# Argmax cross-attention kernel: index of fifteen chunks taken ahead, gathers by row tile, ternary weights in two passes

## The reference, cut to what matters

```python
qp = jnp.einsum('bld,ed->ble', q, Wq)             # 512 rows
scores = jnp.einsum('bld,bmd->blm', qp, kv)       # 512 x 8192
idx = jnp.argmax(scores, axis=-1)
mem = jnp.take_along_axis(kv, idx[..., None], axis=1)
mkv = jnp.einsum('bld,ed->ble', mem, Wkv)
mk, mv = jnp.split(mkv, 2, axis=-1)
...
qh = qp.reshape(b, l, h, dh).transpose(0, 2, 1, 3)
logits = jnp.einsum('bhld,bmd->bhlm', qh, mk) * scale
attn = jax.nn.softmax(logits, axis=-1)
...
def weight_quant(w):
    scale = 1.0 / jnp.clip(jnp.mean(jnp.abs(w)), 1e-05)
    return jnp.clip(jnp.round(w * scale), -1, 1) / scale
```

## Time and profile before

| | before |
|---|---|
| median of 3 runs | 1133.74 us (1131.56 to 1134.1) |
| span of the profiled execution, first to last instruction | 1129.8 us |
| PE busy, share of the span | 1047.0 us, 93% |
| DVE busy | 819.6 us, 73% |
| POOL busy | 416.9 us, 37% |
| share of PE in the chain that ended last | 70% |
| mean granted TensorE clock | 0.980 |

### The profile page before, as it was taken

How to read it: one execution, slowest core, us unless ns; L and a number is a source line. 1 busy time by engine, 2 the same in 40 slices (tenths; PEclk the granted TensorE clock), 3 DMA queues, 4 the chain that set the end, 5 groups by cost and what they waited for, 6 DMA issues and landing times.

```text
span 1129.8 us, 14853 instructions
## 1 busy us (share of the span) xinstructions
PE 1047.0 (93%) x4981; PEld 495.9 (44%) x4981; DVE 819.6 (73%) x1178; ACT 489.2 (43%) x731; POOL 416.9 (37%) x229
## 2 busy tenths in 40 slices
PE   7999999999999989999479999999997799888997
PEld 3444444444444444544134444444642145466453
DVE  5476666799999376685973399999477557476896
ACT  2345554666666537146771110100034615255163
POOL 5177778200000644000020377767128920084003
PEclk9999999999999999999779999999999999999998
DMA  6145545533433345320010435546100010000001
GB/s 237 75 132 194 184 160 166 201 112 121 147 140 112 142 157 224 111 93 1 0 75 6 148 142 200 188 170 188 37 1 1 8 70 1 1 1 1 2 1 38
DMA packets 41830, 112.64 MB, mean 100 GB/s; under 512 B 4512, under 2 KB 15296, under 8 KB 35648
## 3 DMA queue, kind: packets, MB, share of 16 engines
q1 hardware_dynamic: 38592, 101.13, 25.5%
q10 hardware_dynamic: 2880, 9.96, 2.6%
q0 software_dynamic: 320, 1.05, 0.3%
HBM read 103.18 MB, written 7.34 MB: 98 GB/s over the span
## 4 chain that ended last, share of the span: by engine, by line
PE 70%; DVE 17%; ACT 5%; issue 3%; DMA 2%; POOL 2%; DVEq 0%; SPq 0%; ACTq 0%; POOLq 0%
PE PS L773 5%; PE PS L1647 5%; PE PS L1649 5%; PE PS L775 5%; PE PS L1648 5%; PE PS L774 5%; PE PS L804 5%; PE PS L805 5%; PE PS L806 5%; PE PS L255 3%; PE PS L256 3%; PE PS L257 3%; DVE arena L1998 2%; DMA arena<-in_w 2%; DVE arena L1574 2%
## 5 line engine op out<-in xcount | busy, mean ns | idle before, releaser
L773 PE MATMUL PS<-arena 128*128 128x512 f16 x256 | 97.0, 379 | 2.0 <-DVE arena L622 2.0
L1647 PE MATMUL PS<-arena 128*128 128x512 f16 x256 | 97.0, 379 | 1.8 <-DVE arena L1531 1.8
L804 PE MATMUL PS<-arena 128*128 128x512 f16 x256 | 97.0, 379 | 0.9 <-DVE arena L695 0.9
L774 PE MATMUL PS<-arena 128*128 128x512 f16 x256 | 97.0, 379 | 0.0
L775 PE MATMUL PS<-arena 128*128 128x512 f16 x256 | 97.0, 379 | 0.0
L1648 PE MATMUL PS<-arena 128*128 128x512 f16 x256 | 97.0, 379 | 0.0
L1649 PE MATMUL PS<-arena 128*128 128x512 f16 x256 | 97.0, 379 | 0.0
L806 PE MATMUL PS<-arena 128*128 128x512 f16 x256 | 97.0, 379 | 0.0
L805 PE MATMUL PS<-arena 128*128 128x512 f16 x256 | 97.0, 379 | 0.0
L629 DVE TENSOR_TENSOR arena<-PS,arena 128x512 f32<-128x512 f32 x64 | 43.6, 681 | 58.0 <-ACT arena L553 58.0
L249 PE MATMUL PS<-IDENTB 128*128 128x512 bf16 x225 | 60.5, 416 | 21.9 <-DVE SM L1259 21.9
(11 more groups left out here) (370 smaller groups left out, 2439.8 us busy)
## 6 DMA issues: line engine op xcount, KB each, us to landing
arena<-in_ctxT SPq DMA_DIRECT2D x32, 1024.0 KB, 6.3
arena<-in_ctx SPq DMA_DIRECT2D x16, 1024.0 KB, 5.4
arena<-in_w ACTq DMA_DIRECT2D x8, 1024.0 KB, 5.2
arena<-in_w SPq DMA_DIRECT2D x8, 1024.0 KB, 4.8
XN<-in_ffnGU SPq DMA_DIRECT2D x16, 384.0 KB, 3.4
XN<-in_WinT SPq DMA_DIRECT2D x16, 290.0 KB, 5.1
gu_hi<-arena SPq DMA_DIRECT2D x16, 192.0 KB, 3.4
gu_lo<-arena SPq DMA_DIRECT2D x16, 192.0 KB, 3.5
```

The costliest lines, as they stand in the source:

```text
L773: pe.matmul(bank, CHI[:, b, e, cols], QHI[:, e, :], start=(e == 0), stop=False)
L774: pe.matmul(bank, CHI[:, b, e, cols], QLO[:, e, :], start=False, stop=False)
L804: pe.matmul(PS[:, t, :], PHI[:, j, cols], CHI[:, b, j, :], start=False, stop=False)
L1647: pe.matmul(bank, QHI3[:, e, cols], CHI3[:, b, e, :], start=(e == 0), stop=False)
```

## The change

- The last pair of the DVE loop is written out behind it. The reduction over `TOPV` and `TOPI` now takes 15 chunks and stands ahead of the last chunk's maxima. In the last chunk each tile gets its maximum, its place and three operations of one column that merge it with the result of the 15 chunks; each tile then sets a mark of its own.
- POOL issues each tile's gather at that tile's mark. The iota stands ahead of POOL's loop.
- PE no longer waits for the last index with `keep_warm`, which is gone; it waits for the 60th index, and runs 20 fills in four places between the turns and the keys. Turns, keys and values have waits of their own for `s3_idx`, since they write banks that DVE reads.
- The ternary passes are two: the first scales, caps and writes 16-bit integers (which rounds), the second caps at -1 and writes 16-bit floats. The first stands ahead of a b = 0 chunk's maxima, the second behind its first place. SP's wait for `s3_clip` counts one for each piece.

```diff
@@ -234,13 +235,6 @@
                 ins = pe.transpose(PS[:, c, t * P:(t + 1) * P], XN[:, t, c * P:(c + 1) * P], IDENT[:, :])
                 if t == NT - 1:
                     ins.then_inc(xt_psum, 1)
-
-        def keep_warm(pe, bank, rounds):
-
-
-            with pe.Fori(0, rounds):
-                for _ in range(8):
-                    pe.matmul(PS[:, bank, 0:P], IDENT[:, :], ONES[:, :], start=True, stop=True)
 
         def fill(pe, bank, times):
@@ -1322,7 +1316,7 @@
         QST = view(37 * K, [ATT_H, N], F16)
         SHIFT = view(146 * K, [DT, 2, N], F16)
         TRAW = view(154 * K, [2048])
-        TMID = view(162 * K, [2048])
+        TMID = view(162 * K, [2048], I16)
         TOP8 = view(170 * K, [2, NT, 8])
         IDX8 = view(171 * K, [2, NT, 8], U32)
         TOPV = view(172 * K, [NCH, NT])
@@ -1402,7 +1399,7 @@
                 for b in range(2):
                     sp.wait_ge(s3_win_lo, i * 2 + b + 1)
                     sp.dma_start(WINRAW[b], a["WinT"][i * 2 + b]).then_inc(s3_win[b], 16)
-                sp.wait_ge(s3_clip, i * 2 + 1)
+                sp.wait_ge(s3_clip, i + 1)
                 sp.dma_start(TRAW, a["w12"][i]).then_inc(s3_piece, 16)
             for g in range(GROUPS):
@@ -1438,12 +1435,13 @@
         def s3_pool(pool, link):
             pool.sem_inc(s3_hi, AHEAD_SPLIT)
             pool.sem_inc(s3_lo, AHEAD_SPLIT)
-            pool.sem_inc(s3_clip, 2)
+            pool.sem_inc(s3_clip, 1)
             pool.sem_inc(s3_win_lo, 2)
             pool.sem_inc(s3_scores, AHEAD_TILES)
             pool.sem_inc(s3_idx, AHEAD_BANK)
             pool.sem_inc(pool_marks, 1)
             pool.wait_ge(s2_up_psum, F0T)
+            pool.iota(FROM_END, pattern=[[-CH * P, NCH], [0, NT]], base=M, channel_multiplier=0).then_inc(pool_marks, 1)
             with pool.Fori(0, PAIRS) as i:
                 for b in range(2):
                     c = i * 2 + b
@@ -1456,15 +1454,13 @@
                     pool.wait_ge(s3_win_hi, c + 1)
                     pool.tensor_tensor(WINL[:, c, :], WINRAW[b], WINH[:, c, :], ALU.subtract).then_inc(s3_win_lo, 1)
 
-            pool.wait_ge(x_done, NT * 3)
-            pool.iota(FROM_END, pattern=[[-CH * P, NCH], [0, NT]], base=M, channel_multiplier=0).then_inc(pool_marks, 1)
             pool.wait_ge(s3_tern, 8)
-            pool.wait_ge(pool_marks, POOL_MARK["s3_iota"])
-            pool.wait_ge(dve_marks, DVE_MARK["s3_memidx"])
-            for t in range(NT):
+            for t in range(NT):
+                pool.wait_ge(dve_marks, DVE_MARK[f"s3_memidx{t}"])
                 pool.indirect_dma_start(out=MEM[:, t, :], out_offset=None, in_=a["ctx"],
                                         in_offset=bass.IndirectOffsetOnAxis(ap=MEMIDX[:, t:t + 1], axis=0)
                                         ).then_inc(s3_mem[t], 16)
+            pool.wait_ge(s3_win_lo, 4 * DT + 2)
             pool.memset(MKS[96:98, :], MSHIFT).then_inc(pool_marks, 1)
             for n in range(UNITS):
                 g, m, j = n // 16, (n // 4) % 4, n % 4
@@ -1529,39 +1525,73 @@
             for e in range(DT):
                 dve.wait_ge(s3_q_hi, e + 1)
                 dve.tensor_tensor(QLO3[:, e, :], PS[:, 4 + e, :], QHI3[:, e, :], ALU.subtract).then_inc(s3_q_lo, 1)
-            with dve.Fori(0, PAIRS) as i:
+            def tile_max(c, b, t):
+
+                dve.wait_ge(s3_scores, c * CH + t + 1 + AHEAD_TILES)
+                settle(dve)
+                dve.max(TOP8[:, b, t, :], PS[:, b * CH + t, :]).then_inc(s3_max, 1)
+
+            def tile_index(c, b, t):
+
+                dve.wait_ge(s3_max, c * CH + t + 1)
+                settle(dve)
+                return dve.max_index(IDX8[:, b, t, :], TOP8[:, b, t, :], PS[:, b * CH + t, :]).then_inc(s3_idx, 1)
+
+            def ternary_round(i):
+
+                dve.wait_ge(s3_piece, i * 16 + 16)
+                dve.tensor_scalar(TMID, TRAW, W_RECIP[:, bass.ds(i, 1)], 1.0, ALU.mult, ALU.min).then_inc(s3_clip, 1)
+
+            def ternary_clip(i):
+
+                dve.wait_ge(s3_clip, i + 2)
+                dve.tensor_scalar(W12B[:, i, :], TMID, -1.0, None, ALU.max).then_inc(s3_tern, 1)
+
+            def chunk_best(c, b, i=None):
+
+                if i is not None:
+                    ternary_round(i)
+                for t in range(NT + 1):
+                    if t < NT:
+                        tile_max(c, b, t)
+                    if t:
+                        tile_index(c, b, t - 1)
+                    if t == 1 and i is not None:
+                        ternary_clip(i)
+                dve.tensor_copy(TOPV[:, c, :], TOP8[:, b, :, 0])
+                dve.wait_ge(s3_idx, c * CH + CH + AHEAD_BANK)
+                return dve.tensor_copy(TOPI[:, c, :], IDX8[:, b, :, 0])
+
+            with dve.Fori(0, PAIRS - 1) as i:
                 for b in range(2):
-                    c = i * 2 + b
-                    for t in range(NT + 1):
-                        if t < NT:
-                            dve.wait_ge(s3_scores, c * CH + t + 1 + AHEAD_TILES)
-                            settle(dve)
-                            dve.max(TOP8[:, b, t, :], PS[:, b * CH + t, :]).then_inc(s3_max, 1)
-                        if t:
-                            dve.wait_ge(s3_max, c * CH + t)
-                            settle(dve)
-                            dve.max_index(IDX8[:, b, t - 1, :], TOP8[:, b, t - 1, :],
-                                          PS[:, b * CH + t - 1, :]).then_inc(s3_idx, 1)
-                    dve.tensor_copy(TOPV[:, c, :], TOP8[:, b, :, 0])
-                    dve.wait_ge(s3_idx, c * CH + CH + AHEAD_BANK)
-                    dve.tensor_copy(TOPI[:, c, :], IDX8[:, b, :, 0])
-                    if b == 0:
-                        dve.wait_ge(s3_piece, i * 16 + 16)
-                        dve.tensor_scalar(TMID, TRAW, W_RECIP[:, bass.ds(i, 1)], 1.0, ALU.mult,
-                                          ALU.min).then_inc(s3_clip, 1)
-                        dve.wait_ge(s3_clip, i * 2 + 3)
-                        dve.tensor_scalar(TMID, TMID, -1.0, ROUND, ALU.max, ALU.add).then_inc(s3_clip, 1)
-                        dve.wait_ge(s3_clip, i * 2 + 4)
-                        dve.tensor_scalar(W12B[:, i, :], TMID, ROUND, None, ALU.subtract).then_inc(s3_tern, 1)
-
+                    chunk_best(i * 2 + b, b, i if b == 0 else None)
+            link(chunk_best(NCH - 2, 0, PAIRS - 1))
+
+            done = slice(0, NCH - 1)
             dve.wait_ge(pool_marks, POOL_MARK["s3_iota"])
-            link(dve.tensor_copy(FROM_ENDF, FROM_END))
-            link(dve.tensor_reduce(BEST, TOPV.rearrange("p c t -> p t c"), AX.X, ALU.max))
-            link(dve.tensor_tensor(TOPI, FROM_ENDF, TOPI, ALU.subtract))
-            link(dve.tensor_tensor(TOPV, TOPV, BEST.unsqueeze(1).to_broadcast([P, NCH, NT]), ALU.is_equal))
-            link(dve.tensor_tensor(TOPI, TOPI, TOPV, ALU.mult))
-            link(dve.tensor_reduce(BEST, TOPI.rearrange("p c t -> p t c"), AX.X, ALU.max))
-            dve.tensor_scalar(MEMIDX, BEST, -1.0, float(M), ALU.mult, ALU.add).then_inc(dve_marks, 1)
+            link.note(dve.tensor_copy(FROM_ENDF, FROM_END))
+            link(dve.tensor_reduce(BEST, TOPV[:, done].rearrange("p c t -> p t c"), AX.X, ALU.max))
+            link.note(dve.tensor_tensor(TOPI[:, done], FROM_ENDF[:, done], TOPI[:, done], ALU.subtract))
+            link(dve.tensor_tensor(TOPV[:, done], TOPV[:, done], BEST.unsqueeze(1).to_broadcast([P, NCH - 1, NT]),
+                                   ALU.is_equal))
+            link(dve.tensor_tensor(TOPI[:, done], TOPI[:, done], TOPV[:, done], ALU.mult))
+            link(dve.tensor_reduce(EARLIER, TOPI[:, done].rearrange("p c t -> p t c"), AX.X, ALU.max))
+            link(dve.tensor_scalar(EARLIER, EARLIER, -1.0, float(M), ALU.mult, ALU.add))
+
+            def merge_tile(t):
+
+                col = slice(t, t + 1)
+                dve.wait_ge(s3_idx, (NCH - 1) * CH + t + 1 + AHEAD_BANK)
+                link.note(dve.tensor_tensor(NEWER[:, col], TOP8[:, 1, t, 0:1], BEST[:, col], ALU.is_gt))
+                link(dve.scalar_tensor_tensor(out=STEP_ON[:, col], in0=IDX8[:, 1, t, 0:1], scalar=float((NCH - 1) * CH * P),
+                                              in1=EARLIER[:, col], op0=ALU.add, op1=ALU.subtract))
+                dve.scalar_tensor_tensor(out=MEMIDX[:, col], in0=STEP_ON[:, col], scalar=NEWER[:, col],
+                                         in1=EARLIER[:, col], op0=ALU.mult, op1=ALU.add).then_inc(dve_marks, 1)
+
+            for t in range(NT):
+                tile_max(NCH - 1, 1, t)
+                tile_index(NCH - 1, 1, t)
+                merge_tile(t)
             dve.wait_ge(act_marks, ACT_MARK["s3_mks_hi"])
             dve.scalar_tensor_tensor(out=MKS[64:96, :], in0=PS[64:96, 4, :], scalar=float(DH) ** -0.5,
                                      in1=MKS[64:96, :], op0=ALU.mult, op1=ALU.subtract).then_inc(s3_kv, 1)
@@ -1649,11 +1679,10 @@
```

(18 more changed lines are left out.)

## The result

The changed kernel took 1125.34 us in the median (1123.12 to 1129.42) against 1133.80 for the kernel before: a ratio of 0.9933, 95% interval 0.9909 to 0.9957. Its profiled span is 1121.4 us against 1129.8. In a later comparison, beside two experiments, it took 1124.76 against 1134.15, ratio 0.9915 (0.9897 to 0.9933); one of the 11 executions of the kernel before took 2238.28 us there, at a granted clock of 1.00, and is left out of the ratio as slow, for a cause that is not known.

A forecast was written before the change was run, and what follows sets the result against it. PE, busy 93% of the span, was taken to bound the kernel; only the 20.56 us from last score matmul to first entry could shrink. Entry at 816.87 for 822.16, 5.3 off 1133.74, gave 1128.4 us, range 1124.5 to 1131.8.

The forecast's parts named there:

- rival 1: VectorE in the argmax loop isn't held and keeps up with PE: 9.0 us off, 1124.7; chance 0.12.
- the forecast's mechanism: From loop to first attention entry: VectorE late, PE's fills pacing the end; 5.3 us off, 1128.4; chance 0.55.
- the last index 5 to 6 us behind the loop: Sign after the last score matmul: VectorE finishes the fourth tile's index 5 to 6 us later, at 807.6.
- The loop: Argmax loop, 635.60 to 801.60: stays 166 us, with PE hardly waiting.
- DVE late by POOL's hand: Behind chunk 13, POOL's operations hold VectorE's cast some 4 us; first ternary pass ends at 789.53, VectorE 4.2 late.
- The second pass: Second ternary pass, inside chunk 14's work on VectorE: 1.23 us, bounds 0.6 to 2.8.
- A tile's maximum, place and merge: Last chunk on VectorE: each of four tiles takes 2.39 us (2.3 to 2.5).
- The gathers: POOL issues each gather 0.98 after its index, landing 3.7 later; the last lands at 812.3, against 814.68 before.
- PE's pacing: Behind the loop, PE's fills pace the end by 0.6 us: turn 3 at 812.9, entry at 816.87.
- Rival 2, the clock,: PE's clock falls to 1.2 GHz around 805.5 to 808.9, costing 0.8 to 2.5: 1129.2 to 1130.9; chance 0.16.
- Rival 3: In the last chunk, gathers and merges exclude each other, index 3 is 3.9 later: 2.0 off, 1131.7; chance 0.11.
- Rival 4: PE's clock falls near 805 and stays at 1.2 GHz to the first entries: 2.5 later, 1136.2; chance 0.06.

The follow-up runs named there:

- the sixes: The two runs of six fills ahead of turns 2 and 3; the changed kernel without them took 1122.10 us, ratio 0.9905.
- PE's side alone: The kernel before with only PE's part of the change: no keep_warm, fills in its place, index and gathers as before; 1131.87 us, ratio 0.9991.
- three passes: The changed kernel with the ternary weights in three fp32 passes at the places of the two; 1127.01 us, ratio 0.9944.
- no fills: The changed kernel without any of the 20 fills between the loop and the first entry; 1124.47 us, ratio 0.9914.
- DVE's side alone: The changed kernel with PE's part as before: keep_warm back, no fills; 1133.52 us, ratio 1.0018.
- both edits: The changed kernel with copies as reductions, both ternary passes behind a chunk's first place, and fills of 4, 3, 2, 2; first run 1124.25 us, ratio 0.9910.

## Why the prediction was right, and where its sizes were off

The sign, the range (1124.5 to 1131.8) and most of the steps held; the size was short. 5.3 us were forecast, 8.5 measured in the medians, 7.45 of them in the stretch. By its total the run lies nearer to rival 1 (1124.7) than to the forecast (1128.4); that it was the forecast's mechanism shows in the rows alone. Two of the signs named for it did not come: the last index 5 to 6 us behind the loop (3.72), and the entry 15.3 behind it (13.11).

- **The loop.** PE busy in all of it, as said; no wait was added.
- **DVE late by POOL's hand.** The first pass was put at an end of 789.53, from chunk 12's rows moved by one chunk; it ended at 789.48. The cast was held 3.84 us (4.03 in the earlier trace rows). With reductions for the copies and the first pass moved, the lateness is gone by the last tile, whose maximum (801.51 in that run) waits 0.20 for its scores; so the cause is shown. Rival 1, DVE not held, is out. The Trainium skill's "SBUF — State Buffer", section "Who interferes with whom", also says that tensor_reduce does not contend; the reduction of 0.16 beside POOL's L1453 agrees.
- **The second pass** was the first mis-sized term: 1.23 taken from the nearest row, 0.67 measured. The Trainium skill's "VectorE: DVE Perf Modes", section "The perf-mode tier table", gives 0.693 for 2048 elements of bf16; the pass, from 2-byte integers to 16-bit floats, agrees with it.
- **A tile's maximum, place and merge** was the second: 2.39 taken, 2.05 measured (797.07 to the next maximum at 799.12). The waits between dependent operations were 0.15 or less (0.17 each were put), and the one-column operations overlap. Together with the pass, every index came earlier than put, the last at 805.34 in place of 807.6. I had it 1.7 us later than before; it is 0.55 earlier.
- **The gathers.** 0.98 from index to issue holds for the first (0.96: 799.21 to 800.17), and not behind it: the fourth went out 0.26 us behind its index (805.34 to 805.60). Landing took 3.3 to 3.8, 3.7 kept.
- **PE's pacing.** With the data that much earlier, turn 1 didn't wait either, so PE's own row of turns, keys and fills ran from turn 0 on: turn 3 at 810.59 in place of 812.9, entry at 814.73 in place of 816.87. From turn 3 to the entry it was 4.14, 3.97 kept. That the fills pace the end was put at 0.6; taking the sixes out gave 1.76. The step was right and, as the data came earlier, larger.
- **Rival 2, the clock,** stayed out of the changed kernel (1.00 in the stretch) but was near: 1.78 us more lateness brought it in. Its price as put, 0.8 to 2.5, held in that run (1.6).
- **Rival 3** is out: the merge at 800.77 took 0.16 while POOL issued a gather from 800.17 to 801.47.
- **Rival 4** is not what happened, but PE's side alone is its picture: half clock from some 806 to 816, and a stretch 2.1 longer than before.
- The remaining 1.0 us of the medians is not explained by the stretch. In the two profiles it lies in the last 220 us, which the change does not touch (222.37 us from 907.43 on before, 221.40 from 900.00 on after). It is within the scatter: from the entry to the last instruction it was 306.7 us in this profile of the changed kernel and 309.2 in its later one, and 305.6 to 309.2 in all 13 profiles.

## What to carry to other kernels

Where a chain of engines and a run of filler matmuls end together, shorten both or neither: each side of this change alone was worth nothing here, and one of them lost the clock. Before moving small vector operations, look at when an engine that holds them up (here POOL) works; a copy of four columns, held up to 4 us, decided how late this engine was; writing it as a reduction and moving the long passes freed the engine by 1.4 us at the last index. Once the data comes earlier, the fillers that covered the old wait become the path: cut them to the waits that are left.

## What the runs showed of the hardware

The first gather, behind a wait of POOL of 11.78 us, went out 0.96 us after its index and its issue took 1.30; one behind a wait of 1.09 went out after 0.26 and took 0.94. With all gathers in a row, behind a wait of 17.89, the issues took 1.30, then 0.95 or 0.96.

PE's clock fell behind a wait of 3.41 us (three passes), and behind one of 2.46 with another of 0.85 after it (no fills: 1.00 from 808.50 to 810.00, 0.50 from 811.00 to 812.00). The clock did not fall behind 1.65 in the changed kernel or 2.30 in the kernel before, nor behind 3.31 with DVE's side alone, where the whole stretch has 1.00. So the length of a wait alone does not tell; what else does, these runs leave open.

Whole times scatter by some 6 to 7 us, for the kernel before as for the changed one, with stretches that repeat to 0.1. Of the 13 profiles, ten have the loop's end at 801.1 to 802.2 and three (no fills, three passes, the first run with both edits) at 806.1 to 807.3, with the same instructions ahead of stage 3. These three are late from the first 50 us on, where the change has no instruction. PE's timeline there, behind a wait for DVE, first in the changed kernel, whose loop ends at 801.62, with the slice of 10 us around it (columns of the first table):

```profile
41.82 0.39 PE L767 MATMUL PS<-arena 128*128 128x512 f16 x1 [2.05 <-DVE arena L616]
42.04 0.38 PE L768 MATMUL PS<-arena 128*128 128x512 f16 x1
...
40.00:50.00 10.00, 8.18 (x38) 3.74 (x39) 6.28 (x11) 2.44 (x5) 2.96 (x2) 1.00 0.01 2
```

And the first run with both edits, whose loop ends at 807.29:

```profile
43.55 0.60 PE L767 MATMUL PS<-arena 128*128 128x512 f16 x1 [2.02 <-DVE arena L616]
43.95 0.63 PE L768 MATMUL PS<-arena 128*128 128x512 f16 x1
...
40.00:50.00 10.00, 7.98 (x27) 2.96 (x26) 3.56 (x7) 2.04 (x3) 1.48 (x1) 0.83 0.01 2
```

The same instructions stand behind the same wait of 2.0 us, once at full clock and once at half. The mean of this slice is 0.83 in all three late executions and 1.00 in the ten others. The wait alone can't be the cause, then; what makes the clock fall there in some executions is not known. This run is 1.7 us late at these matmuls already and 5.7 late well ahead of the change's first instruction (an operation of ScalarE, L1130, starts at 557.9 in place of 552.2).

So an edit worth 1 us is read from its stretch, and a total of a few runs can hide it.
